# Non-local attention over 8 images on one core: value matmuls in eight high then eight low, sums read by ScalarE and normalised by GpSimd, the projection to g beside the low-half matmuls

## The chip, the cores and the metric

One NeuronCore of a Trainium2 chip runs the whole program. The metric is the device time of one execution in microseconds (us).

## The reference

x is float32, 8 x 128 x 32 x 32; an image has N = 1024 positions of C = 128 channels, Ci = 64.

```
g, theta, phi = 1x1 convolutions of x (128 -> 64 channels) with bias
att = softmax(theta . phi over positions)         # 1024 x 1024 per image
y   = att . g                                     # 1024 x 64
out = x + batchnorm(w_out . y + b_out)            # 1x1 convolution 64 -> 128
```

## The kernel before

The work is cut into 64 tiles of 128 query positions, 8 per image, and into 16 halves of 4 tiles. Every engine runs its own list of instructions in a fixed order, written as a function `step(it, k)` for k = 0, 1, 2, ...; `j = k % 8` is the step within an image, and semaphores tie the lists together. `run_steps` unrolls the first steps, loops over bodies of 16 and unrolls the rest.

Float32 accuracy comes from splitting values into a high and a low part. For the scores, theta and phi lie stacked as high and low rows (`theta_hl`, `phi_hh`, `phi_ll`), so that each tile takes four matmuls of 512 columns (L718) into one of two PSUM pairs `ps_scores`. VectorE takes the row maximum (L584), ScalarE the exponential with the row sum (L542) into `probs`. The scores of tile t wait for the probabilities of tile t-2, since they reuse the PSUM pair (L714).

The probabilities must be turned so that the key position lies on the partitions. Three tiles of four are turned by TensorE: eight 128x128 transposes into `ps_flip` (L784), which ScalarE reads as float16 `pt_hi` (L530) and VectorE as the rest `pt_lo` (L683). The transposes of the next tile wait for `pt_lo`, which frees `ps_flip`. The tile in slot 1 of each half goes another way: GpSimd splits it into `p_hi` and `p_lo` (L404, L407) and SP turns both by transposing DMAs (`turn_hi`, `turn_lo`). The last half is all TensorE's.

The value sum of a half is `weighted_sum` (L727): for the key tiles m, full-width matmuls of `g_parts` (64 high and 64 low columns) with `pt_hi` (L733), and half-width ones, in which only g's 64 high columns meet `pt_lo`, alternating between the two halves of the array (L737). It runs in two portions per half, four full-width and four half-width matmuls at j % 4 == 3 and four and four at j % 4 == 1. VectorE then reads `ps_y`, times `y_unit` and the reciprocal row sums (`scale_y`, L601); the sums reach `inv_all` through DRAM, by SP (`inv_to_row`, `inv_to_all`). TensorE convolves (L745) at j % 4 == 2 and VectorE adds the residual (L594).

For the next image, TensorE projects theta and phi at j = 0 and 1 (L809), g at j = 3 (L824), and transposes g at j = 4 (L831). All of these and the convolution share the one bank `ps_misc`, so each waits until the one before has been read. ScalarE copies them out (L512, L517, L482), GpSimd splits `qk` into `hi` and `lo` (L428, L433), and six DMAs of SP restack these (`restack`, L288); the first scores of the next image wait for the six. The greatest |g| is spread over the partitions by a matmul (L724, j = 7) and scales g. GpSimd also makes `resid` from x (L449), after the store that frees it, and splits the x after next (L458, L463). SP's list per image is `image` (L329).

## Time and profile before

| | |
|---|---|
| three runs, median (lowest to highest) | 223.66 us (220.01 to 224.14) |
| the profiled execution: its own time, its span | 221.7 us, 219.9 us |
| TensorE matmul busy | 207.6 us, 94% |
| VectorE busy | 182.6 us, 83% |
| ScalarE busy | 146.4 us, 67% |
| GpSimd busy | 130.2 us, 59% |
| mean granted TensorE clock | 0.992 |
| DMA | 31.61 MB, 144 GB/s |

The span runs from the first to the last instruction. PE is TensorE (PEld its weight loads), DVE is VectorE, ACT ScalarE, POOL GpSimd, SP the queue that issues most DMAs. Matmuls overlap, and their ends are modelled; the distance from one start to the next is what counts.

### The profile page before, as it was taken

How to read it: one execution, taken by the hardware profiler on the slowest of the kernel's cores; microseconds unless marked ns; L12 is line 12 of the kernel's file. 1: busy time of each engine (PE TensorE's matmuls, PEld its weight loads, DVE VectorE, ACT ScalarE, POOL GpSimd, SP SyncE). 2: the span in 40 equal slices, each digit the busy share in tenths (PEclk: the TensorE clock that was granted, in tenths of full speed). 3: DMA queues.
4: the chain of work that ended last, by engine and by line, in shares of the span. 5: the costliest groups of instructions: out<-in, count | busy, mean ns of one | idle time of the engine just before them, and what ended most of it. 6: DMA issues, size and time to landing. Idle time of an engine off the chain costs nothing.

```text
span 219.9 us, 3935 instructions
## 1 busy us (share of the span) xinstructions
PE 207.6 (94%) x1108; PEld 128.2 (58%) x1108; DVE 182.6 (83%) x298; ACT 146.4 (67%) x266; POOL 130.2 (59%) x113
## 2 busy tenths in 40 slices
PE   7998949999999999999999999999999999999984
PEld 6684627546564756636575656637585565656542
DVE  0789957959999599968999599977999599989871
ACT  2787935748596666748696685758596685767731
POOL 2549854892579564892769754893859342743310
PEclk9999979999999999999999999999999999999999
DMA  5125990699519994399717974299924975165102
GB/s 161 72 92 110 227 195 0 148 213 256 105 50 234 172 252 110 107 192 251 167 48 204 231 208 104 80 226 249 154 72 93 222 213 95 51 127 114 48 3 95
DMA packets 44716, 31.61 MB, mean 144 GB/s; under 512 B 35616, under 2 KB 36128, under 8 KB 44704
## 3 DMA queue, kind: packets, MB, share of 16 engines
q1 hardware_dynamic: 44416, 31.34, 61.9%
q10 hardware_dynamic: 288, 0.14, 0.2%
q8 instruction: 5, 0.08, 0.2%
q14 instruction: 7, 0.06, 0.1%
HBM read 8.36 MB, written 4.23 MB: 57 GB/s over the span
## 4 chain that ended last, share of the span: by engine, by line
PE 71%; DVE 10%; issue 6%; DMA 4%; ACT 3%; SPq 3%; POOL 2%; DVEq 0%; ACTq 0%
PE ps_scores L718 19%; PE ps_flip L784 17%; PE ps_y L733 12%; PE ps_y L737 7%; PE ps_misc L809 4%; DVE pt_lo L683 4%; PE ps_misc L745 3%; PE ps_misc L824 3%; DVE resid L594 3%; DVE neg_max L584 3%; ACT pt_hi L530 2%; DMA phi_ll<-lo 2%; PE ps_scores L757 2%; SPq L288 2%; DMA w_tp<-w_tp_t_dram 2%
## 5 line engine op out<-in xcount | busy, mean ns | idle before, releaser
L542 ACT ACTIVATE probs<-ps_scores,neg_max 128x1024 f32<-128x1024 f32 x64 | 71.8, 1122 | 20.6 <-DVE neg_max L584 20.5
L584 DVE TENSOR_REDUCE neg_max<-ps_scores 128x1 f32<-128x1024 f32 x64 | 77.8, 1216 | 3.3 <-PE ps_scores L718 3.3
L683 DVE SCALAR_TENSOR_TENSOR pt_lo<-ps_flip,pt_hi 128x512 f16<-128x512 f32 x98 | 63.0, 684 | 17.9 <-ACT pt_hi L530 17.5
L530 ACT ACTIVATE pt_hi<-ps_flip 128x512 f16<-128x512 f32 x98 | 53.5, 599 | 35.9 <-PE ps_flip L784 35.7
L784 PE MATMUL ps_flip<-ident,probs 128*128 128x128 f32 x392 | 52.9, 277 | 1.3 <-DVE pt_lo L683 1.0
L784 PEld LDWEIGHTS ps_flip<-ident,probs 128*128 128x128 f32 x392 | 42.9, 141 | 14.9 <-issue 9.6
L718 PE MATMUL ps_scores<-phi_hh,theta_hl 128*128 128x512 f32 x128 | 46.1, 441 | 4.2 <-DMA phi_ll<-lo 2.8
L718 PE MATMUL ps_scores<-phi_ll,theta_hl 128*128 128x512 f32 x128 | 40.4, 397 | 0.0
L404 POOL TENSOR_SCALAR p_hi<-probs 128x1024 f16<-128x1024 f32 x15 | 15.7, 1045 | 31.2 <-ACT probs L542 31.1
L407 POOL TENSOR_TENSOR p_lo<-probs,p_hi 128x1024 f16<-128x1024 f32 x15 | 32.4, 2157 | 1.8
L733 PE MATMUL ps_y<-pt_hi,g_parts 128*128 128x512 f16 (+1 forms) x128 | 33.3, 383 | 0.0
L718 PEld LDWEIGHTS ps_scores<-phi_hh,theta_hl 128*128 128x128 f32 x128 | 19.5, 192 | 15.8 <-ACT probs L542 11.5
L718 PEld LDWEIGHTS ps_scores<-phi_ll,theta_hl 128*128 128x128 f32 x128 | 24.3, 190 | 5.7
L733 PEld LDWEIGHTS ps_y<-pt_hi,g_parts 128*128 128x128 f16 x128 | 10.4, 99 | 19.9 <-issue 12.4
L737 PE MATMUL ps_y<-pt_lo,g_parts 128*64 128x512 f16 (+1 forms) x128 | 19.7, 388 | 0.0
L411 POOL TENSOR_SCALAR g_parts<-g_raw,g_factor 128x512 f16<-128x512 f32 x7 | 4.8, 691 | 23.9 <-DVE g_factor L659 23.9
L463 POOL TENSOR_TENSOR x_lo<-x_in,x_hi 128x512 fp32r<-128x512 f32 x14 | 17.9, 1280 | 0.8
L433 POOL TENSOR_TENSOR lo<-qk,hi 128x512 fp32r<-128x512 f32 x14 | 17.8, 1295 | 0.8
L601 DVE SCALAR_TENSOR_TENSOR y_norm<-ps_y,y_unit,inv_all 128x512 f32<-128x512 f32 x15 | 17.2, 1148 | 1.2 <-PE ps_y L737 1.2
L745 PE MATMUL ps_misc<-y_norm,wout 128*128 128x512 f32 x30 | 15.8, 608 | 0.5 <-DVE y_norm L601 0.5
L542 ACT ACTIVATION_READ_ACCUMULATOR probs<-ps_scores,neg_max 128x1 f32 x64 | 13.5, 210 | 0.0
L737 PEld LDWEIGHTS ps_y<-pt_lo,g_parts 128*64 128x64 f16 x128 | 4.7, 108 | 13.7 <-issue 13.6
(83 smaller groups left out, 179.1 us busy)
## 6 DMA issues: line engine op xcount, KB each, us to landing
x_in<-x_in_dram SPq DMA_DIRECT2D x16, 256.0 KB, 3.1
inv_all<-inv_row SPq DMA_DIRECT2D x15, 256.0 KB, 3.7
out_dram<-resid SPq DMA_DIRECT2D x15, 256.0 KB, 3.3
phi_hh<-hi SPq DMA_DIRECT2D x14, 256.0 KB, 4.9
phi_ll<-lo SPq DMA_DIRECT2D x14, 256.0 KB, 4.5
theta_hl<-hi SPq DMA_DIRECT2D x7, 256.0 KB, 4.0
theta_hl<-lo SPq DMA_DIRECT2D x7, 256.0 KB, 4.1
pt_hi<-p_hi SPq DMA_TRANSPOSE x15, 3.3
```

The costliest lines, as they stand in the source:

```text
L407: nc.gpsimd.tensor_tensor(low[:, :], p[:, :], high[:, :], ALU.subtract).then_inc(p_lo_ready, 1)
L433: nc.gpsimd.tensor_tensor(lo[:, cols], qk[:, cols], hi[:, cols].bitcast(F32), ALU.subtract).then_inc(lo_ready, 1)
L463: nc.gpsimd.tensor_tensor(x_lo[:, cols], x_in[r][:, cols], x_hi[:, cols].bitcast(F32), ALU.subtract).then_inc(x_lo_ready, 1)
L530: nc.scalar.activation(pt_hi[ring][:, c * HALF_TILES:(c + 1) * HALF_TILES, slot * P:(slot + 1) * P], ps_flip[c][:, :].rearrange("p (a n) - ...
L542: nc.scalar.activation(probs[k % PROB_RING][:, :], ps_scores[k % 2][:, :], ACT.Exp, bias=neg_max[:, k % STEPS:k % STEPS + 1], accum_out=ro ...
L584: nc.vector.tensor_reduce(out=top, in_=ps_scores[k % 2][:, :], op=ALU.max, axis=AX.X, negate=True).then_inc(row_max_ready if by_dma(it, k) ...
L683: nc.vector.scalar_tensor_tensor(out=pt_lo[ring][where], in0=ps_flip[c][:, :].rearrange("p (a n) -> p a n", n=P), scalar=PROB_SCALE, in1=p ...
L718: last = nc.tensor.matmul(ps_scores[k % 2][:, cc], theta_hl[r][:, cols], phi[:, cc], start=(n == 0), stop=(n == 1))
L733: nc.tensor.matmul(target[:, to], g[:, m, :], pt_hi[ring][:, m, cols], start=(m == 0), stop=False, skip_group_check=True)
L737: last = nc.tensor.matmul(target[side * CI:(side + 1) * CI, to], g[:, m, 0:CI], pt_lo[ring][:, m, cols], start=False, stop=(m >= MT - 2), ...
L745: nc.tensor.matmul(target, wout[:, 0:C], y_norm[:, cols], start=True, stop=True).then_inc(conv_ready, 1)
L784: last = nc.tensor.transpose(ps_flip[c][:, a * P:(a + 1) * P], probs[(k - 2) % PROB_RING][:, m * P:(m + 1) * P], ident[:, :])
```

## The change

- The 16 value matmuls of a half become eight full-width ones (`sum_high`, at j % 4 == 3) and eight half-width ones (`sum_low`, at j % 4 == 1 of the following half). `sum_high` waits for the turned high part alone (`hi_moved`), `sum_low` for the low part (`lo_moved`).
- `ps_y` is read by ScalarE into a new buffer `y_raw` (times `y_unit`), ahead of its `pt_hi` at j % 4 == 2; GpSimd multiplies by `inv_all` into `y_norm`.
- The convolution moves from j % 4 == 2 to behind `sum_high` at j % 4 == 3, the residual to the step after that.
- The projection to g moves from j = 3 to j = 5, ahead of `sum_low`, its transposes from j = 4 to j = 6, ScalarE's copies to j = 6 and 7; the peak of g is taken and spread in j = 0, 2 and 3 of its own image, by a transpose into `ps_y`; GpSimd makes `g_parts` at j = 5.
- GpSimd does `hi` and `lo` before `p_hi` and `p_lo`, which move one step later; the last part of the x split and `resid` move to j = 0.
- SP issues all six restacks together, the turned tiles around the stores.
- VectorE unrolls 16 steps ahead of its loop instead of 8.

Not shown in the diff: new buffers and semaphores, the waits renamed in `turn_hi` and `turn_lo`, and the removed `scale_y`.

```diff
@@ -58,7 +58,7 @@
-MOVED = 32 * len(BY_DMA)
+MOVED = 16 * len(BY_DMA)
...
@@ -331,29 +334,28 @@
         b, r = image_at(it, k), (k // MT) % 2
         inv_to_row(2 * b - 1)
+        turn_hi(MT * b - HALF_TILES + BY_DMA[0])
         store(it, k - 2 * MT + HALF_TILES)
+        turn_lo(MT * b - HALF_TILES + BY_DMA[0])
         if exists(b + 2, B):
             sp.wait_ge(g_ready, b + 1)
             sp.wait_ge(resid_ready, b + 1)
             load_x(b + 2, r)
-        turn_hi(MT * b + BY_DMA[0])
         inv_to_all(2 * b - 1)
-        turn_lo(MT * b + BY_DMA[0])
         if exists(b + 1, B):
             sp.wait_ge(hi_ready, b + 1)
             restack(theta_hl[1 - r], 0, hi, 0, 1 - r)
             restack(phi_hh[1 - r], 0, hi, CI, 1 - r)
             restack(phi_hh[1 - r], CI, hi, CI, 1 - r)
-        store(it, k - MT)
-        inv_to_row(2 * b)
-        if exists(b + 1, B):
             sp.wait_ge(lo_ready, 2 * b + 2)
             restack(theta_hl[1 - r], CI, lo, 0, 1 - r)
             restack(phi_ll[1 - r], 0, lo, CI, 1 - r)
             restack(phi_ll[1 - r], CI, lo, CI, 1 - r)
+        inv_to_row(2 * b)
+        turn_hi(MT * b + BY_DMA[0])
+        store(it, k - MT)
+        turn_lo(MT * b + BY_DMA[0])
         inv_to_all(2 * b)
-        turn_hi(MT * b + HALF_TILES + BY_DMA[0])
-        turn_lo(MT * b + HALF_TILES + BY_DMA[0])
     for it in range(B // 2):
         image(it, 0)
@@ -396,17 +398,42 @@
-        if exists(t, TILES) and by_dma(it, k - 1):
-            ring, n = ring_of(k - 1), BY_DMA.index((k - 1) % HALF_TILES)
-            p, high, low = probs[(k - 1) % PROB_RING], p_hi[ring][n], p_lo[ring][n]
+        h = half_at(it, k - 10)
+        if k % HALF_TILES == 2 and exists(h, HALVES - 2):
+            normalise_y(h, (k - 10) // HALF_TILES % 2,
+                        it * (8 * STEPS // HALF_TILES) + 16 * ((k - 10) // MT + 1))
+        if tile_is(it, k, TILES + 1):
+            normalise_y(HALVES - 2, 0, 8 * HALVES)
+        if j == 2 and exists(b + 1, B):
+            hold(proj_out, 2 * b + 2)
+            if not is_first(b):
+                hold(stacked[r], it * 16 * STACKS + 16 * STACKS * ((k // MT + 1) // 2))
+            nc.gpsimd.tensor_scalar(out=hi[:, :], in0=qk[:, :], scalar1=1.0, scalar2=0.0,
+                                    op0=ALU.mult, op1=ALU.add).then_inc(hi_ready, 1)
+        if j == 3 and exists(b + 1, B):
+            hold(hi_ready, b + 1)
+            for c in range(PER_IMAGE):
+                cols = slice(c * BANK, (c + 1) * BANK)
+                nc.gpsimd.tensor_tensor(lo[:, cols], qk[:, cols], hi[:, cols].bitcast(F32),
+                                        ALU.subtract).then_inc(lo_ready, 1)
+        t = tile_at(it, k - 2)
+        if exists(t, TILES) and by_dma(it, k - 2):
+            ring, n = ring_of(k - 2), BY_DMA.index((k - 2) % HALF_TILES)
+            p, high, low = probs[(k - 2) % PROB_RING], p_hi[ring][n], p_lo[ring][n]
-            hold(pt_moved[ring], moved_by(it, k - 1) - MOVED)
+            hold(hi_moved[ring], moved_by(it, k - 2) - MOVED)
-            hold(p_hi_ready, move_at(it, k - 1) + 1)
+            hold(p_hi_ready, move_at(it, k - 2) + 1)
+            hold(lo_moved[ring], moved_by(it, k - 2) - MOVED)
-        if j == 0 and exists(b, B) and not is_first(b):
+        if j == 5 and exists(b, B) and not is_first(b):
@@ -414,33 +441,19 @@
-        if j == 1 and exists(b, B) and not is_first(b):
-        if j == 2 and exists(b + 1, B):
-            hold(proj_out, 2 * b + 2)
-            if not is_first(b):
-                hold(stacked[r], it * 16 * STACKS + 16 * STACKS * ((k // MT + 1) // 2))
-            nc.gpsimd.tensor_scalar(out=hi[:, :], in0=qk[:, :], scalar1=1.0, scalar2=0.0,
-                                    op0=ALU.mult, op1=ALU.add).then_inc(hi_ready, 1)
-        if j in (3, 4) and exists(b + 1, B):
-            cols = slice((j - 3) * BANK, (j - 2) * BANK)
-            hold(hi_ready, b + 1)
-            nc.gpsimd.tensor_tensor(lo[:, cols], qk[:, cols], hi[:, cols].bitcast(F32),
-                                    ALU.subtract).then_inc(lo_ready, 1)
-        if j == 5 and exists(b + 2, B):
-            hold(g_ready, b + 2)
+        if j == 6 and exists(b + 2, B):
+            hold(proj_ready, 2 * b + 2)
-        if j == 7 and exists(b + 2, B):
-            split_x(b + 2, r, 2)
-        if j == 1 and exists(b, B):
+        if j == 0 and exists(b + 1, B) and not is_first(b):
+            split_x(b + 1, 1 - r, 2)
+        if j == 0 and exists(b, B):
@@ -448,6 +461,15 @@
+    def normalise_y(h, half, spread):
+        hold(inv_spread[half], spread)
+        hold(y_raw_ready, h + 1)
+        hold(conv_ready, h)
+        nc.gpsimd.tensor_tensor(y_norm[:, :].rearrange("c (t p) -> c t p", p=P),
+                                y_raw[:, :].rearrange("c (t p) -> c t p", p=P),
+                                inv_all[half][:, :].rearrange("c (p t) -> c t p", t=HALF_TILES),
+                                ALU.mult).then_inc(y_scaled, 1)
@@ -481,6 +503,12 @@
+    def evacuate_y(h, r):
+        act.wait_ge(y_ready, h + 1)
+        wait(act, y_scaled, h)
+        nc.scalar.activation(y_raw[:, :], ps_y[:, :], ACT.Copy,
+                             scale=y_unit[:, r:r + 1]).then_inc(y_raw_ready, 1)
@@ -512,10 +540,17 @@
-        if j == 4 and exists(image + 1, B):
+        h = half_at(it, k - 10)
+        if j % HALF_TILES == 2 and exists(h, HALVES - 2):
+            act.wait_ge(y_unit_ready, image_at(it, k - 10) + 1)
+            evacuate_y(h, (k - 10) // MT % 2)
+        if tile_is(it, k, TILES + 1):
+            evacuate_y(HALVES - 2, 1)
+        if j == 6 and exists(image + 1, B):
-        if j == 5 and exists(image + 1, B):
+        if j == 7 and exists(image + 1, B):
@@ -628,28 +653,20 @@
-        h = half_at(it, k - 10)
-        if j % HALF_TILES == 2 and exists(h, HALVES - 2):
-            scale_y(h, (k - 10) // HALF_TILES % 2, (k - 10) // MT % 2, image_at(it, k - 10),
-                    it * (8 * STEPS // HALF_TILES) + 16 * ((k - 10) // MT + 1))
-        if tile_is(it, k, TILES + 1):
-            scale_y(HALVES - 2, 0, 1, B - 1, 8 * HALVES)
-        h = half_at(it, k - 11)
-        if j % HALF_TILES == 3 and exists(h, HALVES - 2):
-            ring, part = (k - 11) // MT % 2, (k - 11) // HALF_TILES % PER_IMAGE
-            dve.wait_ge(resid_ready, image_at(it, k - 11) + 1)
+        h = half_at(it, k - 12)
+        if j % HALF_TILES == 0 and exists(h, HALVES - 2):
+            ring, part = (k - 12) // MT % 2, (k - 12) // HALF_TILES % PER_IMAGE
+            dve.wait_ge(resid_ready, image_at(it, k - 12) + 1)
-        if j == 6 and exists(image + 1, B):
-            peak_of_g(image + 1, (k // MT + 1) % 2)
-        if j == (2 if is_first(image) else 0) and exists(image, B):
+        if j == 0 and exists(image, B) and not is_first(image):
+            peak_of_g(image, k // MT % 2)
+        if j == (2 if is_first(image) else 3) and exists(image, B):
-            spread = ps_y if is_first(image) else ps_misc
-            nc.vector.tensor_reduce(out=g_peak_all[:, r:r + 1], in_=spread[:, 0:P], op=ALU.max,
+            nc.vector.tensor_reduce(out=g_peak_all[:, r:r + 1], in_=ps_y[:, 0:P], op=ALU.max,
@@ -688,7 +705,7 @@
-    run_steps(dve, step)
+    run_steps(dve, step, head=STEPS)
...
@@ -721,24 +738,23 @@
-        nc.tensor.matmul(target, g_peak[:, r:r + 1].to_broadcast([P, P]), ident[:, :],
-                         start=True, stop=True).then_inc(g_peak_spread, 1)
-    def weighted_sum(quarters, ring, r, target, to, cols):
-        g = g_parts[r]
-        tiles = tuple(range(2 * quarters[0], 2 * quarters[-1] + 2))
-        for m in tiles:
-            nc.tensor.matmul(target[:, to], g[:, m, :], pt_hi[ring][:, m, cols],
+        nc.tensor.transpose(target, g_peak[:, r:r + 1].to_broadcast([P, P]),
+                            ident[:, :]).then_inc(g_peak_spread, 1)
+    def sum_high(ring, r, target, to, cols):
+        for m in range(MT):
+            nc.tensor.matmul(target[:, to], g_parts[r][:, m, :], pt_hi[ring][:, m, cols],
-        for m in tiles:
+    def sum_low(ring, r, target, to, cols):
+        for m in range(MT):
-            last = nc.tensor.matmul(target[side * CI:(side + 1) * CI, to], g[:, m, 0:CI],
+            last = nc.tensor.matmul(target[side * CI:(side + 1) * CI, to], g_parts[r][:, m, 0:CI],
-        if quarters[-1] == HALF_TILES - 1:
-            last.then_inc(y_ready, 1)
+        last.then_inc(y_ready, 1)
@@ -799,8 +815,7 @@
-                if not is_first(image):
-                    pe.wait_ge(g_peak_read, image + 1)
+                wait(pe, result_ready, 2 * image - 2)
@@ -809,23 +824,19 @@
-        h = half_at(it, k - 10)
-        if j % HALF_TILES == 2 and exists(h, HALVES - 2):
-            if more:
-                pe.wait_ge(*((proj_out, 2 * image + 2) if j == 2 else (g_out, image + 2)))
-            else:
-                wait(pe, result_ready, h)
-            convolve(h, ps_misc[:, :], slice(0, BANK))
-        if j == 3 and more:
-            wait(pe, proj_out, 2 * image + 2)
+        if j == 2 and exists(image, B) and not is_first(image):
+            pe.wait_ge(y_raw_ready, 2 * image - 1)
+            spread_peak(image, k // MT % 2, ps_y[:, 0:P])
+        if j == 5 and more:
+            pe.wait_ge(proj_out, 2 * image + 2)
-        if j == 4 and more:
+        if j == 6 and more:
@@ -835,40 +846,50 @@
-            if quarter == 0:
-                pe.wait_ge(pt_lo_ready, 2 * flip_at(it, k - 6 + HALF_TILES))
-                pe.wait_ge(pt_moved[ring_of(k - 6)], moved_by(it, k - 6))
+            ring, r = ring_of(k - 6), (k - 6) // MT % 2
+            if quarter == 1:
+                pe.wait_ge(pt_lo_ready, 2 * flip_at(it, k - 7 + HALF_TILES))
+                pe.wait_ge(hi_moved[ring], moved_by(it, k - 6))
-                wait(pe, y_scaled, h)
-            if quarter % 2 == 1:
-                weighted_sum((quarter - 1, quarter), (k - 6) // HALF_TILES % 2, (k - 6) // MT % 2,
-                             ps_y, slice(0, BANK), slice(0, BANK))
+                wait(pe, y_raw_ready, h)
+                if j == 3 and not is_first(image):
+                    pe.wait_ge(g_peak_read, image + 1)
+                sum_high(ring, r, ps_y, slice(0, BANK), slice(0, BANK))
+            if quarter == 3:
+                pe.wait_ge(lo_moved[ring], moved_by(it, k - 6))
+                sum_low(ring, r, ps_y, slice(0, BANK), slice(0, BANK))
+        h = half_at(it, k - 11)
+        if j % HALF_TILES == 3 and exists(h, HALVES - 2):
+            if more:
+                pe.wait_ge(*((proj_out, 2 * image + 2) if j == 3 else (g_out, image + 2)))
+            else:
+                wait(pe, result_ready, h)
+            convolve(h, ps_misc[:, :], slice(0, BANK))
-        if j == 7 and more:
-            wait(pe, result_ready, 2 * image)
-            spread_peak(image + 1, (k // MT + 1) % 2, ps_misc[:, 0:P])
-        if tile_is(it, k, TILES - 2):
+        if tile_is(it, k, TILES - 1):
-            pe.wait_ge(pt_moved[0], moved_by(0, LAST_HALF - HALF_TILES))
+            pe.wait_ge(hi_moved[0], moved_by(0, LAST_HALF - HALF_TILES))
-            pe.wait_ge(y_scaled, HALVES - 2)
-        for tile, quarters in ((TILES - 2, (0,)), (TILES - 1, (1, 2)), (TILES, (3,))):
-            if tile_is(it, k, tile):
-                weighted_sum(quarters, 0, 1, ps_y, slice(0, BANK), slice(0, BANK))
+            pe.wait_ge(y_raw_ready, HALVES - 2)
+            sum_high(0, 1, ps_y, slice(0, BANK), slice(0, BANK))
+        if tile_is(it, k, TILES):
+            pe.wait_ge(lo_moved[0], moved_by(0, LAST_HALF - HALF_TILES))
+            sum_low(0, 1, ps_y, slice(0, BANK), slice(0, BANK))
-    whole = tuple(range(HALF_TILES))
-    weighted_sum(whole, 1, 1, ps_y, LAST_PIECES[0], LAST_PIECES[0])
+    sum_high(1, 1, ps_y, LAST_PIECES[0], LAST_PIECES[0])
+    sum_low(1, 1, ps_y, LAST_PIECES[0], LAST_PIECES[0])
-    weighted_sum(whole, 1, 1, ps_scores[0], slice(0, P), LAST_PIECES[1])
+    sum_high(1, 1, ps_scores[0], slice(0, P), LAST_PIECES[1])
+    sum_low(1, 1, ps_scores[0], slice(0, P), LAST_PIECES[1])
```

## Rows read from the trace of the kernel before

**Rows 1.** Windows, one image: PE, PEld, DVE, ACT, POOL busy (count), clock, DMA share, GB/s.
```profile
95.78:120.75 24.97, 24.58 (x133) 15.01 (x133) 22.02 (x36) 17.50 (x33) 17.03 (x15) 1.00 0.74 174
```
**Rows 2.** Timeline of TensorE, steps of one image: start us, us, engine, line, operation [idle before].
```profile
109.43 0.49 PE L724 MATMUL ps_misc<-ident,g_peak 128*128 128x128 f32 x2
109.75 1.04 PE L784 MATMUL ps_flip<-ident,probs 128*128 128x128 f32 x8
...
114.77 1.04 PE L733 MATMUL ps_y<-pt_hi,g_parts 128*128 128x512 f16 x4
115.73 0.62 PE L737 MATMUL ps_y<-pt_lo,g_parts 128*64 128x512 f16 x4
116.29 1.09 PE L784 MATMUL ps_flip<-ident,probs 128*128 128x128 f32 x8
...
119.21 0.72 PE L718 MATMUL ps_scores<-phi_hh,theta_hl 128*128 128x512 f32 x2
...
120.75 1.08 PE L824 MATMUL ps_misc<-x_in,wg 128*64 128x512 f32 x4 [0.34 <-DVE resid L594]
...
125.14 0.60 PE L831 MATMUL ps_misc<-ident,g_channels 128*128 128x128 f32 x4
125.57 1.04 PE L784 MATMUL ps_flip<-ident,probs 128*128 128x128 f32 x8
```
**Rows 3.** Timeline of TensorE in the last two halves.
```profile
203.71 1.03 PE L745 MATMUL ps_misc<-y_norm,wout 128*128 128x512 f32 x2
204.58 0.59 PE L733 MATMUL ps_y<-pt_hi,g_parts 128*128 128x512 f16 x2
...
212.61 1.46 PE L733 MATMUL ps_y<-pt_hi,g_parts 128*128 128x384 f16 x8
214.00 0.84 PE L737 MATMUL ps_y<-pt_lo,g_parts 128*64 128x384 f16 x8
214.78 0.62 PE L733 MATMUL ps_scores<-pt_hi,g_parts 128*128 128x128 f16 x8
```
**Rows 4.** Waits of the whole span: who, for whom, us in total, times, longest.
```profile
PEld ps_scores L718 <- ACT probs L542: 11.5, 13, 1.3
```
**Rows 5.** Timeline of ScalarE in step 2 of the same image.
```profile
116.98 1.08 ACT L530 ACTIVATE pt_hi<-ps_flip 128x512 f16<-128x512 f32 x2 [1.19 <-PE ps_flip L784]
...
118.95 0.21 ACT L542 ACTIVATION_READ_ACCUMULATOR probs<-ps_scores,neg_max 128x1 f32 x1
```
**Rows 6.** Groups of instructions: count, busy us, mean ns, idle before.
```profile
L433 POOL TENSOR_TENSOR lo<-qk,hi 128x512 fp32r<-128x512 f32 x14 | 17.8, 1295 | 0.8
L601 DVE SCALAR_TENSOR_TENSOR y_norm<-ps_y,y_unit,inv_all 128x512 f32<-128x512 f32 x15 | 17.2, 1148 | 1.2 <-PE ps_y L737 1.2
...
L512 ACT ACTIVATE qk<-ps_misc,vec 128x512 f32<-128x512 f32 x14 | 9.8, 700 | 0.4 <-PE ps_misc L809 0.4
```
**Rows 7.** Timeline of TensorE in the last image, steps 4 and 5.
```profile
196.24 1.09 PE L784 MATMUL ps_flip<-ident,probs 128*128 128x128 f32 x8
...
198.40 1.16 PE L784 MATMUL ps_flip<-ident,probs 128*128 128x128 f32 x8
199.32 0.71 PE L718 MATMUL ps_scores<-phi_hh,theta_hl 128*128 128x512 f32 x2
```
**Rows 8.** Timeline of TensorE at the start, first scores of the second image.
```profile
30.33 1.19 PE L718 MATMUL ps_scores<-phi_hh,theta_hl 128*128 128x512 f32 x2 [2.83 <-DMA phi_ll<-lo]
```
**Rows 9.** Timeline of GpSimd at the start.
```profile
15.69 1.05 POOL L404 TENSOR_SCALAR p_hi<-probs 128x1024 f16<-128x1024 f32 x1 [2.11 <-ACT probs L542]
16.82 2.36 POOL L407 TENSOR_TENSOR p_lo<-probs,p_hi 128x1024 f16<-128x1024 f32 x1
```
**Rows 10.** Timeline of the SP queue at the start.
```profile
24.80 2.04 SPq L288 DMA_DIRECT2D phi_ll<-lo  x2
```
**Rows 11.** Windows, the stretch after that wait (columns as in rows 1).
```profile
29.97:33.40 3.43, 3.07 (x7) 1.64 (x8) 0.99 (x1) 1.17 (x2) 0.49 (x1) 0.50 0.91 167
```
**Rows 12.** DMA issues: what, queue, count, KB each, median us to landing.
```profile
out_dram<-resid SPq DMA_DIRECT2D x15, 256.0 KB, 3.3
```

20 lines of the change are left out of this document (7 added, 13 removed).

## The prediction

> **What bounds the kernel now.** I read the window of one image first: TensorE has matmuls in flight for 24.58 of 24.97 us at full clock, VectorE for 22.0, ScalarE for 17.5 and GpSimd for 17.0 [rows 1]. TensorE sets the pace, so a change gains only by taking work or waits out of TensorE's own order of instructions, and loses by every hole that it opens there. So the second view is TensorE's timeline, by start times [rows 2]. I call step j of an image the work for k = 8b + j: flips of tile k-2 (0.80), scores of tile k+1 (1.0), then what else is hung in. What the reader is to see is what ends step 2: the flips start at 116.29, and the scores of the next tile at 119.21, 2.92 later. The work between is 0.85 + 1.01 + 0.87 (the convolution costs 0.87 where nothing waits behind it [rows 3]), 2.73 in all. The rest, 0.2, is a wait for the probabilities, and the list of waits has it 13 times, nearly twice per image [rows 4]. ScalarE shows why [rows 5]: the two evictions pt_hi begin 0.69 after the first flip, the exponential follows, and its sum is read by 119.16; the scores start 0.05 later, since they need that tile's PSUM pair. So steps 2 and 6 last 2.92 whatever TensorE has to do in them, and the convolution now lies almost wholly inside that time.
>
> **The change, part by part**, per image in the steady state.
>
> Value matmuls 8 + 8. Each pair "high four, low four" pays for entering and leaving the half-width form. High: four of 512 columns last 0.96 and eight of 384 last 1.39 [rows 2, 3], which makes 0.21 per 512 and 0.11 fixed. Low: four last 0.56 and eight of 384 last 0.78, which makes 0.11 fixed too. The flips behind a low group take 0.85, not 0.80. One pair instead of two per half saves 0.11 + 0.11 + 0.05 = 0.27; two halves: **-0.54**. The projection to g is half-width too; next to the low group it saves one leaving and one entering, **-0.15** (0 if float32 to float16 drains as well, 0.2 at most).
>
> The wait before g goes: at 119.21 + 1.03 TensorE was free, g began at 120.75 after the residual on VectorE. Now g stands in step 5, after the residual of step 4: **-0.50**. The peak's spread (109.43 to 109.75) becomes a transpose in step 2, inside the hole: **-0.32**. The g transposes (0.43, 125.14 to 125.57) leave step 4, **-0.43**, for step 6, inside its hole.
>
> The convolutions leave steps 2 and 6 for 3 and 7, behind the eight high matmuls, where nothing covers them: 2 x 0.87 = **+1.74**. The holes do not shrink, since ScalarE's chain is what it was: flips, two pt_hi, exponential. Now the reading of ps_y stands ahead of it on ScalarE. VectorE had the sum 0.2 after the flips began, so ScalarE can start it there, and the nearest row with a per-partition operand (L512) takes 0.70, next one after 0.6 [rows 6]: it ends 0.78 after the first flip where pt_hi used to start at 0.69. That is 0.09 each, **+0.18**; with the price of a plain eviction (half of the 1.08 for two, [rows 5]) it is 0, and 0.5 each if it starts late. The Trainium skill (ScalarE: Activation LUTs, Rules for kernel authors) budgets 0.3 us plus 0.83 ns per element with such an operand, 0.72 us here; by it the term would be 0.2, and the row of 0.70 agrees. In step 6 the copy to g_channels also stands ahead of pt_hi, at the 0.48 spacing of such evictions: **+0.48**.
>
> Step 4 loses its filling (g transposes), so the flips of step 5 must wait for both pt_lo of step 4. The trace has this once, in the last image: flips at 196.24, next flips 198.40, next scores 199.32, 3.08 against 2.66 of plain work [rows 7]: **+0.40**. In step 3 the high matmuls wait until VectorE has read the spread peak out of ps_y; by VectorE's order (a row maximum of 1.22 and the 0.28 read behind it) it is done about 1.1 after the scores of step 3 start, which last 1.04: **+0.10** (0 to 0.5).
>
> VectorE loses 1.15 per half [rows 6] and has no wait of its own added. GpSimd gains one product of 128x512 per half; no row has its stepped operands, so L433 (1.30, [rows 6]) is taken, with 0.7 and 2.6 as ends. Behind it on GpSimd are hi, lo, p_hi, p_lo. It starts when ScalarE is done (0.8 into step 2), ends at about 2.1, and the convolution wants it at 3.0 + 1.04 + 1.72 = 5.8: 3.7 spare, so it costs nothing; without that cover each us late would be a us per half. hi and lo then end near 5.7, and the six restacks that SP now issues together have until step 7 (15.9): hidden. SP's turned tiles, moved ahead of and behind stores, are wanted 5 us or more after they land; hidden too.
>
> Sum per image: -0.54 - 0.15 - 0.50 - 0.32 - 0.43 + 1.74 + 0.18 + 0.48 + 0.10 + 0.40 = **+0.96**. Six images (1 to 6): +5.8.
>
> Start. Now GpSimd splits tile 1 first (15.69 to 19.2) and then makes hi and lo; the last restack is issued at 24.80 to 26.84 and TensorE waits for it until 30.33 (2.83 idle; by start times, a modelled end lying 0.2 behind the next start, it was free at 27.3), after which its clock is at the half level (0.50, 1.2 GHz) up to 33.40 [rows 8 to 11]. With hi and lo first, lo ends 3 us earlier and the restack lands by 27. Late next is TensorE's own order: g and its transposes, now in steps 5 and 6, add 1.4 to 27.3, so the scores start near 28.7: -1.6. If the clock then stays up, the 3.1 us at half level need half that, -1.5. Together -3.1 (0 to -4).
>
> End. The last image has no g; its steps 4 and 5 already have the wait of 3.08. It has one convolution more in the open, the evictions 0.18, and its step 1 saves like the others; the last half but one needs ScalarE and then GpSimd where VectorE took 1.15, but its sum is finished earlier: +0.3 (-1 to +1.5).
>
> Sum: +5.8 - 3.1 + 0.3 = **+3.0** on a span of 219.9; the profiled execution's own time is 221.7, so 224.7 by it. The median of the runs is 223.66 (220.01 to 224.14), 2.0 above that execution, and 226.7 by it. I take the middle: **225.8 us**, own range 221 to 230.
>
> **Rivals.** (B) TensorE's work alone sets the time: the holes of steps 2 and 6 close, because the probabilities come earlier with VectorE relieved. For it: ScalarE waits for row maxima elsewhere. Against: in both steps ScalarE's releaser is the flip, not VectorE [rows 5]. Then the two convolutions, 0.18, 0.48 and 0.40 cost nothing and the two waits of 0.2 go: 0.96 - 2.8 - 0.4 = -2.2 per image, -13.4 in all, with the start some 207 to 210; with one hole closed, 216.
>
> (C) Slower: GpSimd becomes the bound. Its place is the product for the convolution, behind resid, which waits until the store of the image two before has landed. That store is issued 1.0 into step 0 at the earliest and lands 3.3 later [rows 12], then resid 1.1: it ends just before step 2. It decides once GpSimd is late by 3.7; were the product 2.6 us instead of 1.3 and the store 6 us instead of 3.3, it would be 0.3 past that, and with the contention that the DMA share of 0.74 allows, 1 to 2 us an image: 225 + 6 to 12, some 234. GpSimd's busy time of 17.0 + 2.6 in 25.9 speaks against it.
>
> (D) The change does not save what it says: the restack still comes late at the start (GpSimd or the queue), and g beside the low group drains anyway: +3.1 + 0.9, 229.8.
>
> **How the numbers follow.** Forecast 0.60, B 0.16, C 0.14, D 0.10. The range 216.5 to 231 holds the forecast, D and the near edge of B, and leaves out the full B and C. A measurement of this kernel can tell about 2% from no change: 219.2 and 228.1. Slower by more: C, most of D, and a quarter of the forecast (the ends of the evictions and of the peak's read): 0.14 + 0.07 + 0.13 = 0.34. Faster: B and a little of the forecast's low side: 0.17. Within: 0.49.
>
> **What would show it.** In the changed profile: first flips to next scores still 2.9 to 3.0 in step 2 and 3.4 to 3.5 in step 6, with TensorE idle there about 1 us each and waiting for the probabilities; the convolution straight behind eight high matmuls; 3.0 from the flips of step 4 to the scores of step 5; no idle and no half clock near 30; an image taking 25.9. I am wrong if step 2 is under 2.5, if the idle time before scores is small, or if the convolution waits for GpSimd.

## The result and the profile after

| | before | after |
|---|---|---|
| median of 4 runs (lowest to highest) | 222.62 us (220.01 to 224.14) | 227.89 us (227.78 to 230.06) |
| ratio, 95% interval | | 1.0307 [1.0245, 1.0369] |
| profiled execution: own time, span | 221.7, 219.9 | 227.98, 226.2 |
| TensorE, VectorE busy | 207.6, 182.6 | 202.4, 168.4 |
| ScalarE, GpSimd busy | 146.4, 130.2 | 156.2, 153.1 |

The kernel is slower by 3%: 5.3 us more by the medians, 6.3 by the two profiled spans. The forecast was 225.8 us, +3.0 from this change and most likely no clear difference; the time lies inside the range that was given, but the difference is clear, and by the spans twice as large. TensorE and VectorE have less to do than before, and the kernel takes longer. Medians here and below are over all runs of a kernel, while the ratios use only its fast runs, those within 1.5% of its fastest.

The spans are split at two places that both traces have: the first flips (the transposes of the probabilities on TensorE) of image 1 and the first flips of the last image.

| part | before | after | difference | forecast |
|---|---|---|---|---|
| to the first flips of image 1 | 34.62 | 31.42 | -3.2 | -3.1 |
| images 1 to 6 | 150.30 | 155.19 | +4.9 | +5.8 |
| last image to the end | 34.98 | 39.6 | **+4.6** | **+0.3** |

First the images. The window over one of them, from its first flips to the next image's, is to be read beside [rows 1], and the timeline of TensorE in it beside [rows 2]. The columns are the same as there.

```profile
109.01:134.88 25.87, 23.98 (x132) 15.55 (x131) 20.17 (x33) 18.79 (x34) 20.13 (x17) 1.00 0.68 162
```
```profile
115.07 1.09 PE L800 MATMUL ps_flip<-ident,probs 128*128 128x128 f32 x8
...
116.93 0.27 PE L741 MATMUL ps_y<-ident,g_peak 128*128 128x128 f32 x1
118.05 0.73 PE L735 MATMUL ps_scores<-phi_hh,theta_hl 128*128 128x512 f32 x2 [0.84 <-ACT probs L577]
...
119.21 1.89 PE L747 MATMUL ps_y<-pt_hi,g_parts 128*128 128x512 f16 x8
120.93 1.02 PE L761 MATMUL ps_misc<-y_norm,wout 128*128 128x512 f32 x2
121.79 1.04 PE L800 MATMUL ps_flip<-ident,probs 128*128 128x128 f32 x8
...
124.81 0.71 PE L735 MATMUL ps_scores<-phi_hh,theta_hl 128*128 128x512 f32 x2
...
125.92 1.08 PE L835 MATMUL ps_misc<-x_in,wg 128*64 128x512 f32 x4
126.83 1.03 PE L754 MATMUL ps_y<-pt_lo,g_parts 128*64 128x512 f16 x8
127.79 1.09 PE L800 MATMUL ps_flip<-ident,probs 128*128 128x128 f32 x8
...
131.25 0.73 PE L735 MATMUL ps_scores<-phi_hh,theta_hl 128*128 128x512 f32 x2 [1.00 <-ACT probs L577]
```

Three things are to be seen. TensorE has less work in the image (23.98 against 24.58) and 1.9 us in which it does nothing. Steps 2 and 6 are longer than they were (from the flips to the next scores 2.98 and 3.46, against 2.92 in step 2 before), though the convolution has left them: now TensorE idles there for 0.84 and 1.00. These idle stretches are called holes below. And the convolution stands at 120.93, straight behind the eight high matmuls, where its 0.86 is paid in full. ScalarE's own timeline in step 2, beside [rows 5], shows that pt_hi starts 0.75 after the flips instead of 0.69, since y_raw goes first.

```profile
115.23 0.69 ACT L509 ACTIVATE y_raw<-ps_y,y_unit 128x512 f32<-128x512 f32 x1 [0.18 <-issue]
115.82 1.08 ACT L565 ACTIVATE pt_hi<-ps_flip 128x512 f16<-128x512 f32 x2
116.78 1.13 ACT L577 ACTIVATE probs<-ps_scores,neg_max 128x1024 f32<-128x1024 f32 x1
```

The list of waits shows the same over the whole span. TensorE's weight loads wait for the probabilities for 18.2 us, where it was 11.5 [rows 4], and now its matmuls wait too, 14.1 us; the two overlap and don't add up.

```profile
PEld ps_scores L735 <- ACT probs L577: 18.2, 15, 1.4
PE ps_scores L735 <- ACT probs L577: 14.1, 16, 1.0
```

Then the end, which the forecast had nearly free. First TensorE before the change, from the scores of tile 63 on, with the rows that [rows 3] leaves out, and then TensorE after it.

```profile
202.70 0.71 PE L718 MATMUL ps_scores<-phi_hh,theta_hl 128*128 128x512 f32 x2
...
210.04 1.17 PE L784 MATMUL ps_flip<-ident,probs 128*128 128x128 f32 x8 [0.30 <-DVE pt_lo L683]
211.68 1.10 PE L745 MATMUL ps_misc<-y_norm,wout 128*128 128x512 f32 x2 [0.47 <-DVE y_norm L601]
...
215.67 1.13 PE L745 MATMUL ps_scores<-y_norm,wout 128*128 128x384 f32 x4
```
```profile
204.68 0.71 PE L735 MATMUL ps_scores<-phi_hh,theta_hl 128*128 128x512 f32 x2
...
207.50 1.09 PE L800 MATMUL ps_flip<-ident,probs 128*128 128x128 f32 x8 [1.65 <-POOL probs L399]
209.08 2.05 PE L761 MATMUL ps_misc<-y_norm,wout 128*128 128x512 f32 x2 [0.49 <-POOL y_norm L469]
210.92 2.64 PE L747 MATMUL ps_y<-pt_hi,g_parts 128*128 128x512 f16 x8
213.40 1.04 PE L800 MATMUL ps_flip<-ident,probs 128*128 128x128 f32 x8
...
217.96 1.10 PE L761 MATMUL ps_misc<-y_norm,wout 128*128 128x512 f32 x2 [1.29 <-POOL y_norm L469]
...
221.95 1.13 PE L761 MATMUL ps_scores<-y_norm,wout 128*128 128x384 f32 x4
```

GpSimd in the same stretch, and the granted clock in two windows of it (columns as in rows 1):

```profile
202.57 1.12 POOL L399 TENSOR_SCALAR probs<-probs,inv_sum 128x1024 f32<-128x1024 f32 x1 [4.83 <-DVE inv_sum L648]
203.67 0.69 POOL L438 TENSOR_SCALAR g_parts<-g_raw,g_factor 128x512 f16<-128x512 f32 x1
204.34 0.70 POOL L441 TENSOR_SCALAR g_scaled<-g_raw,g_factor 128x512 f32<-128x512 f32 x1
205.19 1.16 POOL L446 TENSOR_TENSOR g_parts<-g_scaled,g_parts 128x512 f16<-128x512 f32 x1
206.33 1.12 POOL L399 TENSOR_SCALAR probs<-probs,inv_sum 128x1024 f32<-128x1024 f32 x1
207.41 1.53 POOL L469 TENSOR_TENSOR y_norm<-y_raw,inv_all 128x512 f32<-128x512 f32 x1
```
```profile
204.70:209.00 4.30, 2.24 (x15) 1.49 (x12) 2.83 (x7) 2.88 (x6) 4.15 (x5) 1.00 0.00 0
209.00:212.40 3.40, 3.32 (x6) 1.26 (x7) 2.02 (x4) 1.37 (x3) 2.16 (x2) 0.50 0.00 0
```

In the last half GpSimd scales the probabilities of each tile before they are flipped. The three operations for g's parts take 2.66 us and are now queued at step 5; they stand between the scaling of tile 60 (202.57) and that of tile 61 (206.33), and GpSimd is busy for 4.15 of 4.30 us. So the flips of tile 61 wait 1.65, the convolution behind them 0.49, and then TensorE runs at the half level (clock 0.50, 1.2 GHz) for 3.4 us: eight high matmuls take 2.48 to the next start instead of 1.72. The convolution at 217.96 waits 1.29 where before it waited 0.47.

### The profile page after: what moved, and what is told of

Same layout as the page of the kernel before. It is cut to its first block, busy times and chain, and to the rows that moved or that the text cites. A ratio compares the mean times of both kernels' runs of the same rounds, so it can differ in the third digit from the quotient of the medians.

```text
span 226.2 us, 3966 instructions
## 1 busy us (share of the span) xinstructions
PE 202.4 (90%) x1100; PEld 131.3 (58%) x1100; DVE 168.4 (74%) x283; ACT 156.2 (69%) x281; POOL 153.1 (68%) x128
## 4 chain that ended last, share of the span: by engine, by line
PE 58%; ACT 15%; issue 11%; DVE 9%; POOL 2%; DMA 2%; ACTq 1%; POOLq 1%; DVEq 0%
PE ps_scores L735 17%; PE ps_y L747 13%; PE ps_flip L800 11%; PE ps_misc L761 6%; ACT probs L577 6%; ACT pt_hi L565 5%; PE ps_misc L824 4%; DVE pt_lo L700 4%; PE ps_misc L835 3%; PE ps_y L754 3%; DVE neg_max L619 3%; DMA vec<-vectors_dram 2%; ACT g_channels L552 1%; POOL probs L399 1%; ACT y_raw L509 1%
## 5 line engine op out<-in xcount | busy, mean ns | idle before, releaser
L577 ACT ACTIVATE probs<-ps_scores,neg_max 128x1024 f32<-128x1024 f32 x64 | 71.8, 1122 | 11.5 <-DVE neg_max L619 10.9
L735 PE MATMUL ps_scores<-phi_hh,theta_hl 128*128 128x512 f32 x128 | 45.7, 438 | 14.7 <-ACT probs L577 14.1
L800 PEld LDWEIGHTS ps_flip<-ident,probs 128*128 128x128 f32 x392 | 43.6, 141 | 24.0 <-issue 14.4
L800 PE MATMUL ps_flip<-ident,probs 128*128 128x128 f32 x392 | 53.5, 277 | 2.9 <-POOL probs L399 1.7
L469 POOL TENSOR_TENSOR y_norm<-y_raw,inv_all 128x512 f32<-128x512 f32 x15 | 23.1, 1542 | 34.7 <-ACT y_raw L509 27.3
L735 PEld LDWEIGHTS ps_scores<-phi_hh,theta_hl 128*128 128x128 f32 x128 | 19.3, 190 | 19.8 <-ACT probs L577 18.2
L747 PE MATMUL ps_y<-pt_hi,g_parts 128*128 128x512 f16 (+1 forms) x128 | 30.6, 383 | 0.0
L629 DVE SCALAR_TENSOR_TENSOR resid<-ps_misc,bn,resid 128x512 f32<-128x512 f32 x15 | 11.3, 751 | 16.7 <-PE ps_misc L761 16.7
L747 PEld LDWEIGHTS ps_y<-pt_hi,g_parts 128*128 128x128 f16 x128 | 11.7, 99 | 17.8 <-issue 6.8
L761 PE MATMUL ps_misc<-y_norm,wout 128*128 128x512 f32 x30 | 16.4, 630 | 1.8 <-POOL y_norm L469 1.8
L754 PE MATMUL ps_y<-pt_lo,g_parts 128*64 128x512 f16 (+1 forms) x128 | 16.5, 379 | 0.0
L462 POOL TENSOR_SCALAR resid<-x_in,bn 128x1024 f32<-128x1024 f32 x8 | 9.0, 1124 | 9.9 <-DMA out_dram<-resid 9.1
L509 ACT ACTIVATE y_raw<-ps_y,y_unit 128x512 f32<-128x512 f32 x15 | 10.3, 689 | 7.5 <-issue 6.8
```

The source lines that it names most:

```text
L469: nc.gpsimd.tensor_tensor(y_norm[:, :].rearrange("c (t p) -> c t p", p=P), y_raw[:, :].rearrange("c (t p) -> c t p", p=P), inv_all[half][: ...
L577: nc.scalar.activation(probs[k % PROB_RING][:, :], ps_scores[k % 2][:, :], ACT.Exp, bias=neg_max[:, k % STEPS:k % STEPS + 1], accum_out=ro ...
L735: last = nc.tensor.matmul(ps_scores[k % 2][:, cc], theta_hl[r][:, cols], phi[:, cc], start=(n == 0), stop=(n == 1))
L747: nc.tensor.matmul(target[:, to], g_parts[r][:, m, :], pt_hi[ring][:, m, cols], start=(m == 0), stop=False, skip_group_check=True)
L754: last = nc.tensor.matmul(target[side * CI:(side + 1) * CI, to], g_parts[r][:, m, 0:CI], pt_lo[ring][:, m, cols], start=False, stop=(m >= ...
L761: nc.tensor.matmul(target, wout[:, 0:C], y_norm[:, cols], start=True, stop=True).then_inc(conv_ready, 1)
```

## The experiments

The theory is that the images lose because ScalarE's chain (flips, reading of PSUM, exponential) keeps the holes of steps 2 and 6 open, and that the end loses because GpSimd has g's parts and the normalisation ahead of what TensorE needs. The rivals are that the images lose by the new path of the sums alone (ScalarE reads them, GpSimd normalises them), and that the end loses by its clock alone. Distances and spans below are of profiled executions, times are medians. "63 to last" is the distance from the scores of tile 63 to the last convolution: 12.97 before (202.70 to 215.67), 17.27 after.

**The changed kernel once more**, the yardstick of the first group.

> The changed kernel itself, on the chip of the three beside it, so that they can be compared with it. Every theory: 1.03 of the kernel before, span near 226.2.

Measured 227.96 (226.34 to 229.66), ratio 1.0276 [1.0181, 1.0372]. The profiled run, 227.85 at a mean clock of 0.992, has the half level at the end again. Two more runs had the same mean clock, so it was presumably there too; the one whose mean clock was 1.0 took 226.34.

**Work put into the holes.**
```diff
+                filler()        # step 2, ahead of the spread of the peak; step 6 too
...
+            def filler():
+                for _ in range(2):
+                    nc.tensor.matmul(ps_y[:, 256:512], ident[:, :], w_tp[:, :], start=True, stop=True)
```


> The changed kernel with extra work: two float32 matmuls of 256 columns (about 0.86 us together) on TensorE in step 2 and in step 6 of images 1 to 7, 14 times 0.86 = 12 us. Their result is used nowhere. Hole theory (in steps 2 and 6 ScalarE's chain flips, y_raw, pt_hi, exponential sets the end, and TensorE idles 0.84 to 1.0): the extra work falls into the idle time, the span grows by 0 to 1 us. Rival (TensorE's work sets the time): +12 us.

**The same work in the open**, the control: steps 3 and 7, ahead of the high matmuls.

> The control: the same two matmuls, but in steps 3 and 7, ahead of the eight high matmuls, where the convolution now stands without cover, 14 times. Hole theory and rival alike: +12 us (0.86 each), less only what the later waits of steps 5 take back (0 to 2).

Measured 226.55 (226.31 to 226.97) in the holes and 239.07 (238.88 to 240.8) in the open. So 12 us of TensorE work cost nothing in one place and 11.1 us over the changed kernel in the other, or 0.2 and 12.7 over that kernel's one run at full clock. By the distances between the spreads of the peak, an image takes 25.74 without the filler, 25.73 with it in the holes and 27.53 with it in the open. The timeline of the first, step 2, shows the filler in place of the idle time and 2.97 from flips to scores, as without it:

```profile
115.67 1.09 PE L804 MATMUL ps_flip<-ident,probs 128*128 128x128 f32 x8
...
117.53 1.02 PE L761 MATMUL ps_y<-w_tp,ident 128*128 128x256 f32 x4
...
118.64 0.73 PE L735 MATMUL ps_scores<-phi_hh,theta_hl 128*128 128x512 f32 x2
```

So work of TensorE that leaves these holes gains nothing. With the filler the kernel was even 1.4 faster than without: its mean clock was 0.998 to 1.0 in all four runs, and no half level showed at the end (63 to last: 15.60). There the last filler stands ahead of the flips of tile 61, whose wait is 0.78 instead of 1.65.

**g's parts one step earlier** in the changed kernel.
```diff
-                if j == 5 and exists(b, B) and not is_first(b):
+                if j == 4 and exists(b, B) and not is_first(b):
```


> The changed kernel with GpSimd's three operations for g_parts in step 4 instead of step 5. Tail theory (in the last image they stand ahead of the scaling of the last tiles: TensorE waits 1.65 for it, then 0.49 for y_norm, and then its clock is at half level for 3.4 us): the flips of tile 61 start 1.5 us earlier, the half clock goes and gives 1.7 back, together -3.2 us, and the images before are as they were. Rival (the tail is long because the last sums go through ScalarE and GpSimd): -0.5 us or nothing.

Measured 225.12 (224.91 to 225.26), 2.8 less. The images are the same (25.74 each); 63 to last is 14.25 instead of 17.27, clock 1.0. On TensorE:

```profile
206.26 1.09 PE L800 MATMUL ps_flip<-ident,probs 128*128 128x128 f32 x8 [0.28 <-POOL probs L399]
207.85 1.10 PE L761 MATMUL ps_misc<-y_norm,wout 128*128 128x512 f32 x2 [0.50 <-POOL y_norm L469]
...
215.06 1.10 PE L761 MATMUL ps_misc<-y_norm,wout 128*128 128x512 f32 x2 [1.28 <-POOL y_norm L469]
```

This splits the end. From that convolution to the flips of tile 62 the changed kernel takes 4.32 (209.08 to 213.40), this one 2.66: the half level costs 1.66. The wait for the scaling costs 1.65 - 0.28 = 1.37. What stays here is the path of the sums: 0.50 and 1.28 - 0.47. It doesn't follow that late parts cost a half level by themselves; the trial that undoes the path of the sums, below, has the wait without the fall.

**Eight high and eight low alone**, in the kernel before.
```diff
-                    if quarter % 2 == 1:
-                        weighted_sum((quarter - 1, quarter), ...)
+                    if quarter == 1:
+                        sum_high(ring, r, ps_y, slice(0, BANK), slice(0, BANK))
+                    if quarter == 3:
+                        sum_low(ring, r, ps_y, slice(0, BANK), slice(0, BANK))
```


> One part of the change alone: the kernel before with the 16 value matmuls of a half as eight high (j % 4 = 3) and eight low (j % 4 = 1), everything else as it was, the convolutions still in steps 2 and 6. Theory (0.27 us per half saved in entering and leaving the half-width form, and nothing lost): 14 or 15 halves, -4 us against the kernel before. Rival (the saving turns into waits elsewhere): -1 to +1 us.

Measured 220.83 (217.53 to 222.15), ratio 0.9944 [0.9877, 1.001]: no proven gain. In the steady images of its trace the distance between two spreads of the peak is 24.77 (61.24 to 185.08, five images) against 25.07 before (59.26 to 184.60): -0.30, not -0.54. The rest went into waits for VectorE: g now waits 0.44 for the residual instead of 0.34, and the convolution of step 6 waits 0.22 for y_norm, whose sum is complete later. The first spread of image 1 comes 2.2 later in this trace than in the one before, since the scores there happened to wait 3.97 instead of 2.83 and the half level followed; that wait varies in kernels with one and the same start (last section).

**The path of the sums alone** (read by ScalarE, normalised by GpSimd) in the kernel before.
```diff
+                if j % HALF_TILES == 2 and exists(h, HALVES - 2):
+                    evacuate_y(h, (k - 10) // MT % 2)          # ScalarE
+                    normalise_y(h, (k - 10) // HALF_TILES % 2, ...)   # GpSimd, same step
-                    scale_y(h, ...)                            # VectorE
```


> Another part alone: the kernel before with the sums read by ScalarE ahead of pt_hi and normalised by GpSimd first thing in steps 2 and 6; value matmuls in four portions and the convolution in steps 2 and 6 as before. Theory: y_norm is done 2.7 us after the flips start instead of 1.35, so the convolution ends at 3.6 to 3.7 and the next scores start there instead of at 2.92: +0.75 per half, +9 to +11 us. Rival (VectorE, relieved of 1.15 per half, lets the rest come earlier): 0 or faster.

Measured 236.8 (234.75 to 239.2), ratio 1.0724 [1.0623, 1.0825]; more than I expected. The trace is of the run of 239.2. With the convolution still in steps 2 and 6 it waits for GpSimd there, 0.66 and 0.70; in step 2 it is 2.67 from flips to convolution, where it was 1.86. And GpSimd splits late what image b+1 needs: hi begins at 102.84, 5.9 behind the flips of step 2, behind y_norm, p_hi and p_lo, so that the low restacks are issued from 108.96 on and the scores of step 7 wait 1.92 for them. Behind that wait four high matmuls take 1.86 to the next start, where 0.96 is full clock [rows 2].

```profile
96.95 1.09 PE L798 MATMUL ps_flip<-ident,probs 128*128 128x128 f32 x8
...
99.62 1.13 PE L759 MATMUL ps_misc<-y_norm,wout 128*128 128x512 f32 x2 [0.66 <-POOL y_norm L465]
```
```profile
115.53 0.73 PE L732 MATMUL ps_scores<-phi_hh,theta_hl 128*128 128x512 f32 x2 [1.92 <-DMA phi_ll<-lo]
```

So this path by itself costs far more than the whole change, which also gives the convolution a later step and hi and lo an earlier place; that it is these two which make the path bearable was not tried by itself.

**The start alone, first try.** GpSimd splits qk ahead of tile 1's probabilities; SP's low restacks stayed behind inv_to_row(0).

> The kernel before with the order of the start alone changed: for image 0 GpSimd makes hi and lo ahead of p_hi and p_lo, and SP issues the six restacks ahead of the two turned tiles. Theory: TensorE no longer waits 2.83 at 30, and its clock is not at half level for the 3.4 us behind (worth 1.5): -3 to -4.5 us. Rival (the wait is the restacks' own length, or something else is late next): -1 us or less.

A miss: 222.65 (220.8 to 224.01), ratio 1.0075 [1.0019, 1.0131], no gain. The low restacks were ready to go but were issued from 22.16 to 23.90, behind an inv_to_row that waits for a sum until 21.77, and the turned tiles right behind them; in the changed kernel the low restacks go out from 19.89 to 21.91. What the scores of image 1 wait for is now the turned low part of tile 1, and the first flips of image 1 come at 35.93, later than the 34.62 before:

```profile
31.50 0.70 PE L737 MATMUL ps_scores<-phi_hh,theta_hl 128*128 128x512 f32 x2 [4.11 <-DMA pt_lo<-p_lo]
```

**The start alone, second try**, with the low restacks ahead of inv_to_row(0) for image 0.
```diff
-                store(it, k - MT)
-                inv_to_row(2 * b)
+                if b > 0:
+                    store(it, k - MT)
+                    inv_to_row(2 * b)
                 if exists(b + 1, B):
                     sp.wait_ge(lo_ready, 2 * b + 2)
...
+                if b == 0:
+                    inv_to_row(0)
+                    turn_hi(MT * b + BY_DMA[0])
+                    turn_lo(MT * b + BY_DMA[0])
```


> The kernel before with the first image's start of the changed kernel and nothing else of it: in image 0 GpSimd splits qk ahead of tile 1's probabilities, and SP issues the high and the low restacks ahead of inv_to_row(0) and of tile 1's two transposing transfers (in the last start trial the low restacks still stood behind inv_to_row(0), and were issued at 22.16 to 23.90). Theory, that the start's gain is the order of the restacks on SP: the low restacks go out at about 20 us, the scores of image 1 don't wait for them (2.83 us in the kernel before), no half clock near 30, first flips of image 1 at 31.0 to 31.8 instead of 34.62: 3.0 us less, 219.3. Rival, that the gain needs the changed kernel's other moves (projection, g parts, later copies of tile 1): no more than 1 us less, 221.5.

Measured 219.11 (218.2 to 231.78, ten runs, the slowest at a mean clock of 0.852), ratio 0.9894 [0.9849, 0.9939]; first flips of image 1 at 32.41, no half level near 30. So the order of the restacks, on GpSimd and on SP together, is 2.2 of the 3.2; GpSimd's part with half of SP's, the first try, gained nothing. The rest is in what the scores wait for now:

```profile
29.57 0.70 PE L739 MATMUL ps_scores<-phi_hh,theta_hl 128*128 128x512 f32 x2 [2.10 <-DMA pt_lo<-p_lo]
```

The kernel before waits for both turned parts of the tile ahead of these scores; the changed one waits for the high part only ahead of the high matmuls and for the low part only ahead of the low ones. There the same scores start at 28.68. That this is the remaining third is read from the trace; it was not tried alone.

**VectorE's residual one step earlier**, ahead of the row maximum, in the kernel before.
```diff
-                if j % HALF_TILES == 3 and exists(h, HALVES - 2):
-                    add_residual(h, ...)
...
+                if j == 2 and exists(h, HALVES - 2):      # and at step 7 as before
+                    add_residual(h, ...)
                 t = tile_at(it, k + 1)
                 if exists(t, TILES):
                     row_maximum(it, k + 1)
```


> The kernel before with VectorE adding the residual of step 2's convolution ahead of the row maximum of that step instead of behind it. Theory: the projection to g in step 3, which waits 0.5 for that residual, starts at once: -0.5 in each of 6 images, -3 us. Rival (the row maximum that is now 0.7 later delays the probabilities and with them the scores): 0 or slower.

Measured 219.87 (217.35 to 221.75), ratio 0.9875 [0.9799, 0.9952], a gain of about 1%. g no longer waits:

```profile
118.90 0.62 PE L723 MATMUL ps_scores<-phi_ll,theta_hl 128*128 128x512 f32 x2
119.46 1.08 PE L829 MATMUL ps_misc<-x_in,wg 128*64 128x512 f32 x4
```

The image gains 0.34 (24.73 against 25.07), the wait that the trace names [rows 2], and not the 0.50 of the forecast.

**g's parts at step 5 alone**, in the kernel before: the three operations of GpSimd at step 5 instead of steps 0 and 1, nothing else.

> The kernel before with the three g parts operations of GpSimd at step 5 instead of steps 0 and 1 and nothing else. Theory, that in the end of the changed kernel these three operations (3.0 us) stand between the scalings of tiles 60 and 61 and make the flips late: the flips of tile 61 about 1.5 us late, from the first flips of the last image to the end 36.5 to 38 instead of 34.98, with half clock behind it up to 38.5; the time 224 to 226. Rival, that the end of the changed kernel is long by its path of the sums (ScalarE, then GpSimd) and the g parts add nothing by themselves: 222.0 to 222.8.

This miss taught most: 222.35, ratio 1.0015 [0.9964, 1.0065]. In the last half g's parts stand on GpSimd where they do in the changed kernel. The scaling of tile 61 begins at 206.25, 1.21 after the scores of tile 63 (1.65 in the changed kernel), and its flips could not have started before 207.4; yet 63 to last is 12.97, as before. TensorE shows why:

```profile
205.04 0.71 PE L718 MATMUL ps_scores<-phi_hh,theta_hl 128*128 128x512 f32 x2
...
206.06 1.02 PE L745 MATMUL ps_misc<-y_norm,wout 128*128 128x512 f32 x2
206.92 0.59 PE L733 MATMUL ps_y<-pt_hi,g_parts 128*128 128x512 f16 x2
...
207.78 1.09 PE L784 MATMUL ps_flip<-ident,probs 128*128 128x128 f32 x8
```

The convolution and a quarter of the value matmuls, 1.72 from start to start, cover the late scaling. In the changed kernel both have moved behind the flips.

**The same with eight and eight**, which leaves the convolution alone as cover.

> The kernel before with eight and eight and with the three g parts operations at step 5: the two parts that met in the changed kernel's end, without its path of the sums. With g parts late alone (last trial) the 2.6 us of convolution and value matmuls between the scores of tile 63 and the flips of tile 61 covered the late scaling. Theory, that this cover is what the change took away: with eight and eight only the convolution (1 us) is left there, the scaling of tile 61 ends at about 4.8 us behind the start of the scores of tile 63 less what moves, and the flips of tile 61 wait 0.3 to 1.2 us; from the scores of tile 63 to the last convolution 13.4 to 14.5 (before 12.97, eight and eight alone 12.78), at half clock up to 1.7 more; the time 221.5 to 223.5. Rival, that late g parts cost nothing without the path of the sums: 12.8 as before, 220.8.

Measured 220.66, ratio 0.9966 [0.9904, 1.0029]; 63 to last 13.37, against 12.78 with eight and eight alone. The time is under the 221.5 to 223.5 expected, and the distance just under its 13.4 to 14.5. The flips wait 0.54:

```profile
200.08 1.10 PE L744 MATMUL ps_misc<-y_norm,wout 128*128 128x512 f32 x2 [0.19 <-DVE y_norm L601]
201.71 1.07 PE L783 MATMUL ps_flip<-ident,probs 128*128 128x128 f32 x8 [0.54 <-POOL probs L397]
```

Here the scaling begins 1.63 after the scores of tile 63, as late as in the changed kernel. The convolution as cover leaves a wait of 0.54; no cover, as in the changed kernel, 1.65.

**The path of the sums undone in the changed kernel**: VectorE normalises from PSUM, all else as changed.
```diff
-                    evacuate_y(h, (k - 10) // MT % 2)      # ScalarE
-                    normalise_y(h, ...)                    # GpSimd
+                    scale_y(h, ...)                        # VectorE, step 2 and 6
```


> The changed kernel with its sums normalised by VectorE in one operation straight from PSUM, as before, and nothing else undone (g, projection, convolutions, g parts and start as changed). Theory: ScalarE's y_raw (0.69) no longer stands ahead of pt_hi and probs in steps 2 and 6, so the waits of 0.84 and 1.00 before the scores shrink by up to 0.69 each, 7 to 8 us over the images, unless VectorE's pt_lo becomes what they wait for; at the end the last-but-one convolution waits 0.5 instead of 1.28; the g parts still cost theirs. 219 to 222. Rival, that the holes come from the empty steps themselves (TensorE's own work left them): 225 to 227.

Measured 222.52 (222.37 to 222.95), ratio 1.0055 [1.0012, 1.0097] where the changed kernel had 1.0276: 5.4 less than it, just outside what I expected, and no different from the kernel before at the 2% bound. It came from two places. The image has 25.34 instead of 25.87 (next scores behind step 6, 104.17 to 129.51), and 63 to last is 14.06 instead of 17.27; the start is 0.3 longer and the last image up to tile 63 0.6. The gain per image is nearly all in step 6: step 2 goes from 2.98 to 2.92, step 6 from 3.46 to 2.92, since the copy to g_channels no longer stands behind a y_raw and is done before the flips. The holes themselves stay:

```profile
104.17 0.73 PE L723 MATMUL ps_scores<-phi_hh,theta_hl 128*128 128x512 f32 x2 [0.47 <-ACT probs L548]
...
116.81 0.72 PE L723 MATMUL ps_scores<-phi_hh,theta_hl 128*128 128x512 f32 x2 [0.80 <-ACT probs L548]
...
205.43 1.09 PE L788 MATMUL ps_flip<-ident,probs 128*128 128x128 f32 x8 [1.63 <-POOL probs L399]
```

The last row is worth a look: it is nearly the wait of the changed kernel, but the convolution behind it doesn't wait, and the clock stays full. So the first rival is half right: without the path of the sums most of the loss is gone, but the image is still 0.29 longer than before. The second rival is wrong, since g's parts moved forward took away a wait as well as the fall. The moves of g, of its transposes and of the peak were not tried alone.

**What is left when only the gaining parts are kept**: the kernel before with eight and eight, the residual earlier in step 2 (at step 6 it stays as before, unlike in the expectations), the peak as a transpose, and the start of the second try; the sums stay with VectorE, g and its parts where they were. The second trial is the same without the start.

> The kernel before with four parts together: eight high then eight low value matmuls, the residual of VectorE at steps 2 and 6 ahead of the row maximum, the spread of the peak as a transpose, and the start of the trial beside this one. VectorE keeps the evacuation of the sums, g stays where it was, g's parts stay at steps 0 and 1. Theory, that what the change lost was the evacuation path and the end, and that these parts gain by themselves: per image -0.30 (eight and eight), -0.34 (residual; with the first perhaps -0.5 together more, since its idle of 0.44 before g goes too), 6 images -4 to -5; peak -0.3 an image at most; start -3; together 213 to 216. Rival, that TensorE's sections only trade waits: 218 to 220.

> As the trial of four parts but without its start: eight and eight, residual at steps 2 and 6, peak as a transpose. Expected 3 us slower than that one: 216 to 219. If it is as fast, the start's order is worth nothing once the steady images are shorter.

Measured 215.07 (214.03 to 216.37) with the start, ratio to the kernel before **0.9723 [0.9657, 0.979]**, and 219.07, 0.9875 [0.9833, 0.9918], without it. Both are near what was expected. The first beats both kernels. Its span is 7.7 shorter than that of the kernel before: 2.9 at the start (flips of image 1 at 31.75), 4.1 in the images (24.37 each on average, against 25.05) and 0.8 at the end. In one image TensorE has matmuls in flight for 23.81 of 24.07, at full clock:

```profile
105.14:129.21 24.07, 23.81 (x133) 15.24 (x131) 21.79 (x36) 17.20 (x32) 17.05 (x14) 1.00 0.73 173
```

## Why the prediction was wrong

**The step that failed is "End: +0.3".** It measured +4.6. Its text priced one convolution in the open, the evictions and the path of the sums, and counted the last half but one as "finished earlier". Up to the scores of tile 63 that is what came, 0.29 more than before; all the rest is behind them. The forecast left out that g's parts, moved from steps 0 and 1 to step 5, pass the scalings of the last half on GpSimd; I had followed GpSimd's order in the steady images and at the start only. From the scores of tile 63 on, the waits add up: 1.65 (scaling) + 0.49 + 1.29 (path of the sums) + 1.66 (half level), less the 0.30 and 0.47 that the kernel before waited there, is 4.32; the distance 63 to last grew by 4.30. The experiments show the scaling and the clock (g's parts one step earlier, -2.8 us), that it takes both the late parts and the lost cover (the two trials of late parts in the kernel before, with waits of 0 and 0.54), and the path of the sums (the trial that undoes it, which also ends the fall). What stays open is what decides the clock: 1.65 and 0.49 close together came ahead of a fall, 1.63 alone and 0.78 with 0.49 (the filler's kernel) did not, and one of the four runs of the changed kernel itself kept full clock.

The Trainium skill (TensorE: Matmul & The Clock Gate, Part 1) says that the half level is the state of an idle engine, and that the number of slow matmuls at the start of one and the same kernel changes from run to run. By that, a fall at the end need not be a fixed cost of the change; the runs agree (mean clock 0.992 in three of four, 1.0 in one).

**The images were right in mechanism, and the sum is 0.14 high.** Forecast +0.96 each, measured 4.9 / 6 = +0.82. The forecast 24.97 + 0.96 = 25.93 for an image came out as 25.87; the other part of the difference is the start value, since the images before average 25.05 and not the 24.97 of the one I had read. Term by term: step 2 2.98 (forecast 3.01); step 6 3.46 (3.49); step 3 from scores to flips 3.74 (3.73); step 4 flips to scores of step 5 3.02 (3.08); g beside the low group saves 0.10 (0.15), from 0.91 in place of 1.01 to the next start. The two terms for the path of the sums, 0.18 + 0.48, were worth 0.53 in the trial that undoes it, and without them the sum is +0.30, where that trial has 25.34 - 25.05 = +0.29. The eight and eight gave only 0.30 alone, not 0.54, since waits for VectorE took the rest; the wait ahead of g was worth 0.34, not 0.50.

**The start was right in its main reason and lucky in its number**: scores of image 1 at 28.68 (forecast 28.7), flips at 31.42, no half level. Two thirds is the order on GpSimd and SP; the other third, the split wait for the turned tiles, was not among my reasons. Nor was TensorE's own order the last limit: its g transposes began at 27.53 and take 0.43, and then it waited 0.56 for probabilities. And the -3.2 is against one trace before; the wait that goes away here was between 2.4 and 4.1 us long in kernels that start as the one before (last section).

**GpSimd's product** takes 1.54 with its stepped operand (15 times), not 1.30. In the images the spare time of 3.7 us covered it, as forecast, and the convolution doesn't wait there. At the end nothing covers it: the sign "if the convolution waits for GpSimd" came true there, 0.49 and 1.29, and only there.

**The rivals.** B (the holes close) fell: 12 us of filler were free. C (GpSimd the bound) is false in the images. In the last half GpSimd does hold TensorE up, but by g's parts and the scaling, not by C's store and resid. D fell: the start's saving came, and g beside the low group saved its 0.10.

**The chances.** With the end at its measured +4.6 the same sum would have been 5.8 - 3.1 + 4.6 = +7.3. That is a span of 227.2, where 226.2 was measured, and a time of 229.0 by the profiled execution or 231.0 by the median, over the bound of 228.1 that I had set for slower. That 225.8 lies only 2.1 from the measured 227.89 is partly luck: by the profiled executions the forecast was 224.7 against 227.98, 3.3 off, and the median of 223.66 that lifted it was 222.62 with a fourth run. (The middle of 224.7 and 226.7 is 225.7, not 225.8.)

## What to carry to other kernels

A wait that another engine's chain sets hides the work that lies in it; moving work out of it gains nothing, and putting work in is free until it is full. When an operation moves in an engine's order, follow that order once more through the first and the last round of the loop, where other work stands beside it, and ask on the waiting engine what lies between as cover: late parts alone cost nothing here, lost cover alone a wait of 0.28 us, and the two together, with the half level that followed, 3 us more. Take a change of several parts apart: here the parts without the new path of the sums and with g left where it was gain 2.8%, while the whole loses 3.1%.

## What the runs showed of the hardware

A product of 128x512 on GpSimd took 1.54 us where one operand is read in steps. Differences of two operands of 128x512 without such steps took 1.16 (float16 result) to 1.30 us (fp32r result); that the steps alone make the difference was not tried.

```profile
L469 POOL TENSOR_TENSOR y_norm<-y_raw,inv_all 128x512 f32<-128x512 f32 x15 | 23.1, 1542 | 34.7 <-ACT y_raw L509 27.3
```

Much of the spread of the kernel before (219.4 to 225.1, one run of 688.05 left out) goes with the clock: its runs of 219.41, 219.47 and 219.98 had a mean granted clock of 1.0, those of 224.71, 224.75 and 225.11 had 0.982 or 0.983. The traces show where it comes from. Seven traces are of kernels with the start of the one before. In them the first scores of image 1 waited 2.37, 2.42, 2.83, 2.98, 3.97, 4.11 and 4.12 us for phi_ll. The half level followed in all but one of them; the wait of 2.42 had none, that of 2.37 had one. The runs with the three long waits had mean clocks of 0.983 or 0.984, the other four 0.992, 1.0, 0.992 and 0.986. The kernels with the other start had no half level there and varied less: the changed kernel without the path of the sums kept 0.997 to 1.0 and ran ten times within 0.6 us.
